# Batch 0's output products of layer 2 with split operands, their weights through the stream, and a new order table from the last head on

## What is computed

```python
q = hidden_states @ Wq                       # layer 1, k and v alike
attn = softmax(q k^T * scaling + band mask)
x = layernorm(x + (attn @ v) @ Wo)
...
scores = jnp.einsum('btd,d->bt', hidden_states, w_router)      # layer 2
_, idx = jax.lax.top_k(scores, k)            # k = 128 of 1024
x = sel.reshape(S, D)                        # S = 2 * 128
h = _rms_norm(x, ln1_w)
q = (h @ wq + bq).reshape(S, N_HEADS, HEAD_DIM)                # 16 heads; kk and v: 8 heads
q = q * cos + _rotate_half(q) * sin
att = softmax(causal(q kk^T / sqrt(128)))
attn_out = (att @ v).reshape(S, N_HEADS * HEAD_DIM) @ wo
x1 = x + attn_out
h2 = _rms_norm(x1, ln2_w)
mlp = jax.nn.silu(h2 @ w_gate) * (h2 @ w_up) @ w_down          # inner width 2048
processed = x1 + mlp
output = hidden_states.at[b, idx].set(gate * processed + (1.0 - gate) * x)
x = layernorm(x + output)
```

## Time and profile before

| | us |
|---|---|
| median of 3 runs | 1269.94 (1269.14 to 1270.07) |
| the profiled execution | 1268.86 |
| its span | 1267.1 |
| TensorE busy | 1252.8 |
| VectorE busy | 807.0 |
| ScalarE busy | 623.2 |
| GpSimd busy | 245.1 |
| moved by transfers | 89.36 MB, 71 GB/s on average |

### The profile page before, as it was taken

The page is one execution under the profiler, slowest core; times in us unless marked ns, Lnnn a source line. Parts: engine busy times, 40 slices in busy tenths (PEclk is TensorE's granted clock), DMA queues, the critical chain, the costliest instruction groups (busy, mean ns, idle before and its releaser), DMA issues.

```text
span 1267.1 us, 19392 instructions
## 1 busy us (share of the span) xinstructions
PE 1252.8 (99%) x7474; PEld 1103.3 (87%) x7474; DVE 807.0 (64%) x2227; ACT 623.2 (49%) x1448; POOL 245.1 (19%) x216
## 2 busy tenths in 40 slices
PE   9999999999999999999999999999999999999997
PEld 8898989898989898988989898989898987568896
DVE  5555665656555655667776776565656579969633
ACT  5544444444544454555554444445444444558653
POOL 2101111020202020024220211111111113310155
PEclk9999999999999999999999999999999999999999
DMA  6000101010101110203320110110010106565563
GB/s 207 28 25 25 43 17 51 17 51 17 50 18 50 34 51 1 84 18 117 109 96 30 34 34 30 60 34 34 18 51 17 51 18 235 167 216 168 182 217 117
DMA packets 62445, 89.36 MB, mean 71 GB/s; under 512 B 3264, under 2 KB 36032, under 8 KB 62352
## 3 DMA queue, kind: packets, MB, share of 16 engines
q1 hardware_dynamic: 61936, 86.82, 20.8%
q0 software_dynamic: 416, 1.31, 0.3%
HBM read 79.20 MB, written 8.91 MB: 70 GB/s over the span
## 4 chain that ended last, share of the span: by engine, by line
PE 94%; DVE 3%; DMA 1%; ACT 1%; POOL 1%; issue 0%; POOLq 0%
PE proj L1170 45%; PE y L1170 14%; PE s L1170 12%; PE o L1170 10%; PE tp L1263 6%; PE proj L1178 2%; DVE arena L1696 1%; PE s L1178 1%; ACT arena L1480 1%; PE o L1178 1%; DMA late<-rope,position 0%; DMA wraw<-in_L_ffn_wq 0%; PE tp L1399 0%; PE y L1377 0%; DMA yacc<-in_L_attn_hidden_states 0%
## 5 line engine op out<-in xcount | busy, mean ns | idle before, releaser
L1170 PE MATMUL proj<-arena 128*128 128x256 f32 (+1 forms) x3504 | 647.3, 333 | 0.1
L1170 PEld LDWEIGHTS proj<-arena 128*128 128x128 f32 x3504 | 535.5, 189 | 60.2 <-DVE arena L1696 1.1
L2045 POOL TENSOR_TENSOR arena<-wraw,arena 128x1024 fp32r<-128x1024 f32 x73 | 174.8, 2402 | 826.8 <-ACT arena L1480 826.7
L1518 ACT ACTIVATE prob<-prob,stat 128x384 f32<-128x384 f32 (+1 forms) x256 | 150.8, 589 | 363.5 <-DVE stat L1731 363.0
L1696 DVE TENSOR_TENSOR arena<-proj,arena 128x512 fp32r<-128x512 f32 (+1 forms) x256 | 142.2, 557 | 239.7 <-ACT arena L1480 237.0
L1170 PE MATMUL y<-arena 128*128 128x512 f32 x816 | 211.6, 394 | 0.0
L1170 PE MATMUL s<-arena 128*128 128x384 f32 (+2 forms) x912 | 203.6, 338 | 0.7 <-DVE arena L1696 0.6
L1696 DVE TENSOR_TENSOR arena<-tp,arena 128x384 fp32r<-128x384 f32 (+2 forms) x258 | 134.8, 522 | 93.2 <-ACT arena L1480 92.4
L1170 PE MATMUL o<-arena 128*128 128x256 f32 (+2 forms) x966 | 191.9, 319 | 0.0
L1480 ACT ACTIVATE arena<-proj 128x512 fp32r<-128x512 f32 (+1 forms) x256 | 124.3, 486 | 130.7 <-PE proj L1170 114.0
L1170 PEld LDWEIGHTS s<-arena 128*128 128x128 f32 x912 | 157.6, 188 | 17.2 <-DVE arena L1696 1.8
(11 more groups left out here) (163 smaller groups left out, 669.4 us busy)
## 6 DMA issues: line engine op xcount, KB each, us to landing
wraw<-in_L_attn_Wv SPq DMA_DIRECT2D x16, 512.0 KB, 3.4
wraw<-in_L_attn_Wo SPq DMA_DIRECT2D x16, 512.0 KB, 3.7
wraw<-in_L_attn_Wq SPq DMA_DIRECT2D x15, 512.0 KB, 3.4
wraw<-in_L_attn_Wk SPq DMA_DIRECT2D x15, 512.0 KB, 3.4
yacc<-in_L_attn_hidden_states SPq DMA_DIRECT2D x16, 256.0 KB, 3.6
y_dram<-yacc SPq DMA_DIRECT2D x16, 256.0 KB, 2.2
out<-works SPq DMA_DIRECT2D x16, 256.0 KB, 2.7
wraw<-in_L_ffn_wq SPq DMA_DIRECT2D x8, 512.0 KB, 4.6
```

Of the source, the lines that this page charges most:

```text
L1170: ins = e.matmul(out_ap, l[a], r[b], start=first and i == 0 and j == 0, stop=final and i == n - 1 and j == 2, skip_group_check=skip)
L1518: e.activation(prob[s][:, 0:n], prob[s][:, 0:n], ACT.Exp, bias=stat[:, 4 * s + 1:4 * s + 2], scale=-1.0, accum_out=stat[:, 4 * s + 2:4 * s ...
L2045: e.tensor_tensor(lo, wraw[n % RAW_SLOTS][:], hi.bitcast(F32), ALU.subtract).then_inc(*G_.inc("wsplit", n, "lo"))
```

## The change

Batch 0's `o2` uses `three_passes`, as batch 1's does. `av2` of batch 0 no longer copies its result whole: ScalarE writes a high part and VectorE a low part, which goes to an oT buffer of layer 1 (`slot1`). The eight pieces of `wo` for batch 0 leave `homely` and stand in the stream as pieces 64 to 71, ahead of batch 1's projections, which are now 72 to 87; batch 1's output weights are 88 to 95 and the MLP 96 to 119. The late slots are handed over when batch 0's last projection is done. The table `LAST` is new from its first entry to its last; the number of splits grows by eight, six of them on VectorE and two on GpSimd.

```diff
--- before.py
+++ after.py
@@ -215,71 +215,73 @@
...
-T.out.15.5 T.rows.1.1 T.p2.0.1 T.p2half.0.2 T.out.15.6 T.out.15.7 T.p2t.0.0 T.p2.0.2 T.p2t.0.1 T.p2half.0.3
...
+T.as2.0.5 T.p2t.0.7 T.av2.0.4 T.as2.0.6 T.o2.0.3 T.at2.0.5 T.rinhs.1 T.as2.0.7 T.o2.0.4 T.av2.0.5 T.p2half.1.0
...
@@ -367,18 +369,18 @@
         q2T = whole(start["q"], NH, NT)
         k2T = whole(start["v"], NKV, NT)
         v2 = whole(start["v"] + NKV * NT, NB, NKV * HD)
-        o2T = whole(start["pT"], NH, NT)
         by_cos = [whole(start["pT"] + NH * NT + i * D, D) for i in range(2)]
         by_sin = whole(start["pT"] + NH * NT + 2 * D, D)
         slot0, slot1, slot2 = (start["oT"] + 2 * i * O_N for i in range(O_SLOTS))
 
 
         hT = [whole(slot2, KT, P), [carve(slot0 + 2 * HD + z * D, KT, P) for z in range(2)]]
-        o2_parts = [carve(start["pT"], NH, NT)[:, :, (1 - z) * P:(2 - z) * P] for z in range(2)]
         p2T = [whole(slot2 + D + i * D, D) for i in range(2)]
         ub = carve(slot2 + 3 * D, 4 * HD)
         rope_late = whole(slot0, 2 * HD)
         h2T = [carve(slot1 + z * KT * NT, KT, NT) for z in range(2)]
+        o2_half = [carve(start["pT"], NH, NT)[:, :, b * P:(b + 1) * P] for b in range(NB)]
+        o2_parts = [[o2_half[0], carve(slot1, NH, P)], [o2_half[1], o2_half[0]]]
         aT = [[carve(start["q"] + (2 * s + z) * NT, NT) for z in range(2)] for s in range(A_SLOTS)]
 
         yacc = sb("yacc", [P, TT, D])
@@ -486,8 +488,7 @@
             as2=dict(T=("made",), V=("max",), S=("exp",)),
             an2=dict(V=("recip",), S=("prob",)),
             at2=dict(T=("made",), S=("copy",)),
-            av2=dict(T=("made",), S=("copy",)),
-            av2s=dict(T=("made",), S=("hi",), V=("lo",)),
+            av2=dict(T=("made",), S=("hi",), V=("lo",)),
             o2=dict(T=("made",)),
             res=dict(V=("sum", "squares"), G=("mean", "rstd")),
             resh=dict(V=("h", "lo", "gated", "mixed"), T=("made",), S=("hi",)),
@@ -554,6 +555,7 @@
                 if G >= 1:
                     stream.append((("o", *divmod(G - 1, NG)), rows(Wo, (G - 1) % NG)))
         stream.append((("o", NB - 1, NG - 1), rows(Wo, NG - 1)))
+        stream += [(("o2", 0, c), rows(wo, c)) for c in range(NH * HD // GW)]
         for n, (which, c) in enumerate(QKV_ORDER):
             stream += [(("p2", 1, n, half), wide(dict(q=wq, k=wk, v=wv)[which], c, half)) for half in range(2)]
         stream += [(("o2", 1, c), rows(wo, c)) for c in range(NH * HD // GW)]
@@ -567,7 +569,6 @@
         homely = []
         for n, (which, c) in enumerate(QKV_ORDER):
             homely += [(("p2", 0, n, half), wide(dict(q=wq, k=wk, v=wv)[which], c, half)) for half in range(2)]
-        homely += [(("o2", 0, c), rows(wo, c)) for c in range(NH * HD // GW)]
         slot_of, closed_by, split_on = {}, {}, {}
         free_slots = [(s, None) for s in range(SPLIT_SLOTS)]
         loaded_to, split_to = [0], [0]
@@ -819,6 +820,10 @@
             job("p2", b, n)
             if b == 0:
                 leave_home(("p2", b, n, 1), "p2", b, n, "made")
+                if n == len(QKV_ORDER) - 1:
+                    for s in range(LATE_SLOTS):
+                        free_slots.append((SPLIT_SLOTS + s, ("p2", 0, n, "made")))
+                    load_next()
             else:
                 retire(("p2", b, n, 1), "p2", b, n, "made")
             yield "p2r"
@@ -855,27 +860,19 @@
             job("an2", b, n)
             yield "at2"
             hold("tp", ("at2", b, n), S_, "at2", b, n, "copy")
-            hold(f"p2T{s}", ("at2", b, n), T_, "av2s" if b else "av2", b, n, "made")
+            hold(f"p2T{s}", ("at2", b, n), T_, "av2", b, n, "made")
             job("at2", b, n)
             yield "av2"
-            hold("o1", ("av2", b, n), *((V_, "av2s", b, n, "lo") if b else (S_, "av2", b, n, "copy")))
-            job("av2s" if b else "av2", b, n)
+            hold("o1", ("av2", b, n), V_, "av2", b, n, "lo")
+            job("av2", b, n)
             yield "o2"
 
             if n == 0:
                 hold("s1", ("o2", b, 0), V_, "res", b, "sum")
-            if b == 1:
-                need("o2", b, n)
+            need("o2", b, n)
             job("o2", b, n)
-            if b == 0:
-                leave_home(("o2", b, n), "o2", b, n, "made")
-            else:
-                retire(("o2", b, n), "o2", b, n, "made")
+            retire(("o2", b, n), "o2", b, n, "made")
             attended.append(b)
-            if (b, n) == (0, NKV - 1):
-                for s in range(LATE_SLOTS):
-                    free_slots.append((SPLIT_SLOTS + s, ("o2", 0, NKV - 1, "made")))
-                load_next()
 
         def residual2(b):
             yield "res"
@@ -1414,19 +1411,12 @@
                     b, c = key
                     if c == 0:
                         pe.wait_ge(*freed("s1", "o2", b, 0))
-                    if b == 0:
-                        w2 = home[home_of[home_number["o2", b, c]]].rearrange("p (k n) -> p k n", k=HG)
-                        pe.wait_ge(*landed("o2", b, c))
-                        pe.wait_ge(*S_.at("av2", b, c, "copy"))
-                        ins = one_pass(e, bank["s1"][:, :], [(o2T[:, 2 * c + h, 0:P], w2[:, h, :]) for h in range(HG)],
-                                       c == 0, c == NKV - 1)
-                    else:
-                        w2 = [z.rearrange("p (k n) -> p k n", k=HG) for z in weights("o2", b, c)]
-                        pe.wait_ge(*split("o2", b, c))
-                        pe.wait_ge(*V_.at("av2s", b, c, "lo"))
-                        ins = three_passes(e, bank["s1"][:, :],
-                                           [([o2_parts[z][:, 2 * c + h, :] for z in range(2)], [w2[z][:, h, :] for z in range(2)])
-                                            for h in range(HG)], c == 0, c == NKV - 1)
+                    w2 = [z.rearrange("p (k n) -> p k n", k=HG) for z in weights("o2", b, c)]
+                    pe.wait_ge(*split("o2", b, c))
+                    pe.wait_ge(*V_.at("av2", b, c, "lo"))
+                    ins = three_passes(e, bank["s1"][:, :],
+                                       [([o2_parts[b][z][:, 2 * c + h, :] for z in range(2)], [w2[z][:, h, :] for z in range(2)])
+                                        for h in range(HG)], c == 0, c == NKV - 1)
                     ins.then_inc(*T_.inc("o2", b, c, "made"))
 
                 elif kind == "gu":
@@ -1646,18 +1636,12 @@
                     act.wait_ge(*T_.at("at2", b, n, "made"))
                     whole_copy(p2T[n % 2][:, 0:w], bank["tp"][:, 0:w], "at2", b, n)
 
-                elif kind == "av2s":
-                    b, n = key
-                    act.wait_ge(*T_.at("av2s", b, n, "made"))
-                    hi_part(o2_parts[0][:, 2 * n:2 * n + 2, :], bank["o1"][:, 0:2 * P].rearrange("p (h q) -> p h q", h=2),
-                            "av2s", b, n)
-
                 elif kind == "av2":
                     b, n = key
                     act.wait_ge(*weighed(NHEADS - 1, TT - 1))
                     act.wait_ge(*T_.at("av2", b, n, "made"))
-                    whole_copy(o2T[:, 2 * n:2 * n + 2, 0:P],
-                               bank["o1"][:, 0:2 * P].rearrange("p (h q) -> p h q", h=2), "av2", b, n)
+                    hi_part(o2_parts[b][0][:, 2 * n:2 * n + 2, :], bank["o1"][:, 0:2 * P].rearrange("p (h q) -> p h q", h=2),
+                            "av2", b, n)
 
                 elif kind == "resh":
                     b, = key
@@ -1929,12 +1913,12 @@
                     b, = key
                     lo_part(hT[1][1], bank[bank_of["rinh", b]][:, :].rearrange("p (k n) -> p k n", k=KT), hT[1][0], "rinhs", b)
 
-                elif kind == "av2s":
+                elif kind == "av2":
                     b, n = key
 
-                    dve.wait_ge(*T_.at("o2", 0, NKV - 1, "made"))
-                    lo_part(o2_parts[1][:, 2 * n:2 * n + 2, :], bank["o1"][:, 0:2 * P].rearrange("p (h q) -> p h q", h=2),
-                            o2_parts[0][:, 2 * n:2 * n + 2, :], "av2s", b, n)
+                    dve.wait_ge(*(T_.at("o2", 0, NKV - 1, "made") if b else T_.at("out", NB * NG - 3, TT - 1, "made")))
+                    lo_part(o2_parts[b][1][:, 2 * n:2 * n + 2, :], bank["o1"][:, 0:2 * P].rearrange("p (h q) -> p h q", h=2),
+                            o2_parts[b][0][:, 2 * n:2 * n + 2, :], "av2", b, n)
 
                 elif kind == "res":
                     b, = key
```

132 lines of the change are left out of this document (67 added, 65 removed).

## The result

The changed kernel takes 1277.76 us (1276.85 to 1280.97, 4 runs), the kernel before 1269.54 in the same session: a ratio of 1.0069 (95% interval 1.0057 to 1.0081), 8.8 us slower by the ratio. Forecast were 1272.2 us and a range of 1267.0 to 1275.8; the time lies above the range. The profiled execution took 1277.35 us, 8.5 more than that of before.

A forecast was written before the change was run, and what follows sets the result against it. TensorE, busy 1252.8 of 1267.1 us, was taken to bound the kernel, with VectorE neck and neck in one stretch. Terms -1.9 + 0.3 + 3.6 - 0.5 + 0 + 0.8 = +2.3 us on the median 1269.94 gave 1272.2, range 1267.0 to 1275.8.

The forecast's parts named there:

- The products: Batch 0's eight output products on TensorE: each 1.47 us split instead of 1.71, a gain of 1.9 us.
- Ranks and prefix: TensorE reaches batch 1's prefix matmuls at 1104.8, VectorE has the ranks at 1105.1: +0.3 us, bounds 0 and 1.7.
- The wait before batch 1's transposes: TensorE runs out of work before batch 1's normalised rows are ready: +3.6 us, bounds 2.7 and 5.4.
- GpSimd's first root operation: In normalising batch 1's rows, a VectorE split beside it makes it take 1.1 us instead of 0.19.
- M: Start of batch 1's prefix matmuls; transposes could start at M + 13.6, TensorE would be there at M + 10.0.
- one burst until 1110.6: Before the change, eight 512 KB output-weight loads issued together just ahead of batch 1's row load, which took 6.0 us.
- The old 0.48: TensorE's existing wait at batch 1's transposes (1121.93) goes: -0.5 us.
- The residual norm: TensorE's 1.08 us wait at batch 0's norm (1137.50): both sides shrink alike, 0 (-1.1 to +0.5).
- Batch 1's attention, with as many splits as before, 0: Batch 1's attention stage keeps its number of weight splits, so it costs 0 us more.
- rival 2: MLP weight stream too slow, over 2.8 us a piece, adding 3 us: +4.5 in all, 1274.4 us; chance 0.25.
- The MLP: The MLP starts two weight pieces poorer, making TensorE wait: +0.8 us (0 to 2.5).
- the gap ahead of the fifth product: In the MLP, late up weights delay an activation whose bank TensorE wants: a wait of 0.8 to 1 us.

The follow-up runs named there:

- half_loads: Changed kernel with loads of stream pieces 72 to 95 bringing only half of each piece (256 KB instead of 512): 1273.58 us, ratio 1.0016.
- raw4: Changed kernel with a fourth raw buffer for batch 1's stage (pieces 75 to 95), all computed: 1275.20 us, ratio 1.0039.
- small_lows: Changed kernel, VectorE making only 128 of 1024 low-part columns for those of pieces 68 to 87 in early buffers: 1275.84 us, ratio 1.0030.
- raw4_root_warm: Changed kernel plus fourth raw buffer, piece 71's split behind the normalised rows, 45 small products in the wait before batch 1's transposes: 1273.35 us, ratio 1.0028.
- raw4_g68: Like raw4_root_warm, but piece 68's low part on GpSimd ahead of its gathers and 25 small products instead of 45: 1273.20 us, ratio 1.0026.

## Why the prediction was wrong, point by point

**The products** (-1.9): right. The pairs between fp32 work took 1110.56 to 1112.03 and 1127.93 to 1129.40, 1.47 each.

**Ranks and prefix** (+0.3, bounds 0 and 1.7): 0. The prefix matmuls ran at 1105.85, where I had 1105.1, since TensorE had lost 0.84 ahead of them at a transpose of the first layer's scores. Part of this is luck: VectorE had the ranks only at 1105.79, so without that 0.84 TensorE would have waited about 0.8 here. That wait, and 0.50 at 1114.01 for an output's low part, no step named.

**The wait before batch 1's transposes** (+3.6, bounds 2.7 and 5.4): 3.59, with GpSimd's first root operation at 1.09, as forecast. Part of this is luck: the chain took 14.7 us from the prefix matmuls where I had 13.6 (the rotary rows held VectorE for 0.84), and TensorE reached it at M + 11.1 where I had 10.0. One reading behind the bounds was wrong too: of the eight loads that I had in one burst until 1110.6, three were issued at 1094.06 and five from 1106.99. **The old 0.48** is gone, as forecast.

**What the wait does to what follows**: missing. I priced the work behind the wait by durations that TensorE has at full clock. It cost 1.55 more at 0.91 of the clock over that stretch.

**The residual norm** (0, -1.1 to +0.5): -0.9, 0.18 instead of 1.08, because TensorE came to it later.

**"Batch 1's attention, with as many splits as before, 0"**: this is the step that failed, and the largest: 1.16 + 1.92 = +3.1 of copies behind late weights. (0.34 at 1149.44, for a rotation on VectorE, belongs to this stage but not to the weights: it stayed at 0.37 in half_loads and raw4.) The number of splits is the same, their supply isn't. I counted instructions per stage and not the stock with which the stage starts. Before, five of batch 1's own pieces were asked for by 1075 while batch 0 took its weights from elsewhere; now eight pieces of batch 0 go through the same three raw buffers first, two of batch 1's are asked for by 1117, and its stage lives from what the ring delivers. I had this mechanism (rival 2), with its price worked out from load, high part and low part, but asked only for the MLP whether it binds. It bound one stage earlier. That load size is worth 6.7 us after the change and next to nothing before it, and that a fourth buffer gives 3.8 back, shows that this supply binds there. How much of its pace is the load and how much VectorE (small_lows, 5.0) isn't shown.

**The MLP** (+0.8, 0 to 2.5): +1.35 (78.44 against 77.09 from its first product to the end), within the bounds, but by luck. ScalarE did wait longer for these weights (13.8 us in all instead of 12.1), yet the gap ahead of the fifth product isn't there: five tiles run through, and the two waits come later, for a low part of GpSimd and a product of VectorE, which no step named.

```profile
1197.16 14.66 PE L1167 MATMUL proj<-arena 128*128 128x256 f32 x120
...
1235.21 1.61 PE L1167 MATMUL s<-arena 128*128 128x512 f32 x6 [0.72 <-POOL arena L2076]
...
1240.15 3.14 PE L1167 MATMUL proj<-arena 128*128 128x256 f32 x24 [0.46 <-DVE works L1952]
```

**The sum.** Of the 6.5 us between +2.3 and +8.8, 3.1 are late weights in batch 1's stage, 0.3 its rotation, 1.55 the clock, 1.3 the two unnamed waits, 0.55 the MLP, less 0.9 at the norm and 0.3 at the ranks; about 0.9 isn't located. By my own test ("wrong would be the whole account if TensorE were idle for more than 1 us at a place that none of these names") the account of the middle was right and that of the stage behind it wrong.

What isn't settled: with ring, root and clock taken care of, 1.0026 to 1.0028 is left, although the products are cheaper. VectorE was busy 17.4 to 18.7 of 20 us in the stretches of 1100 to 1120 and 1120 to 1140 (before 13.3 and 13.7), and each wait taken away there came up elsewhere; that this is VectorE's queue is argued from these traces, not shown by a run of its own.

## What to carry to other kernels

When work is moved onto a shared stream, count the stock with which each later stage starts and the pace of the ring (load, first pass, second pass, over the number of buffers) for every stage behind, not only for the last. A wait whose removal shows at its place but not in the time may be covered by a slower pace behind it: halve a cost of the suspected pace, in the kernel before too, before moving anything by hand. And a wait of some microseconds on TensorE can cost more than its length (3.59 cost 1.55 more here), so price what stands behind it at the lower clock as well.

## What the runs showed of the hardware

The granted clock can fall behind waits shorter than I thought worth a term, and not the same way in each execution. In the execution of small_lows that was profiled TensorE waited 1.95, 1.86 and 2.05 us at 1118, 1138 and 1165, and three stretches in a row were granted less:

```profile
1120.00:1140.00 20.00, 18.14 (x80) 14.57 (x79) 13.00 (x28) 13.31 (x24) 0.74 (x2) 0.93 0.65 211
1140.00:1160.00 20.00, 19.61 (x89) 15.25 (x88) 14.69 (x37) 14.24 (x34) 0.00 (x0) 0.93 0.37 115
1160.00:1180.00 20.00, 17.95 (x86) 14.92 (x85) 12.30 (x34) 15.86 (x37) 0.00 (x0) 0.91 0.58 175
```

That execution had a mean clock of 0.994 and took 1279.25 us; the other five had 0.996 to 0.998 and took 1273.87 to 1276.82. In the changed kernel the wait of 1.92 at 1165 left the clock at 1.00. As an estimate, a mean lower by 0.001 is 1.3 us of 1276. The changed kernel's own runs went from 1276.85 at 0.997 to 1280.97 at 0.994: by this estimate 3.8 of the 4.1 us between them are the clock, twice this change's direct gain. Kept at work through its longest wait (raw4_root_warm), all executions had 0.998.

GpSimd's issue of an indirect load is held up by VectorE as well: it took 2.15 us when a split had started just before it (1109.45 behind 1109.41), and 1.10 in raw4_g68, where it started first (1108.09, the split at 1108.27), as in the kernel before, where no split stood beside it. The Trainium skill, "SBUF — State Buffer", section "Who interferes with whom", says that the order of issue decides which of the two is held up. GpSimd's rows agree; VectorE's split, begun second beside it in raw4_g68, took its usual 1.22 us, so no row here shows VectorE held up.
